# Mixture of experts beside a recurrent scan on one core: gate and up weights made the stationary operand, 256 rows of one expert at a time, loops written out

## What is computed

```python
xn = layernorm(x)
# branch 1: recurrent scan over each sequence
xk, xv, xr = (xn * m + shift(xn) * (1 - m) for m in (mix_k, mix_v, mix_r))
k, v, r = xk @ Wk.T, xv @ Wv.T, sigmoid(xr @ Wr.T)
s = (r * wkv_scan(time_decay, time_first, k, v)) @ Wo.T     # running max, numerator, denominator
# branch 2: 16 experts, 4 per token, FFN width 256
top_w, top_e = top_k(softmax(xn @ w_router.T), 4);  top_w /= sum(top_w)
ffn = sum over the 4 chosen experts e of
      top_w[e] * ((silu(xn @ w_gate[e]) * (xn @ w_up[e])) @ w_down[e])
out = x + s * silu(ffn)
```

## Time and profile before

| | us |
|---|---|
| median of 3 runs | 352.96 |
| the runs | 349.82, 352.96, 354.08 |
| span of the profiled execution | 358.9 |
| PE busy in it | 304.6 (85%) |
| DVE busy | 274.4 (76%) |
| POOL busy | 223.9 (62%) |
| ACT busy | 149.9 (42%) |

### The profile page before, as it was taken

One profiled execution on the slowest core, in us unless ns is written; L12 is line 12 of the kernel. 1 busy time (PEld: TensorE's weight loads), 2 busy tenths in 40 slices (PEclk: granted clock), 3 DMA queues, 4 the chain that ended last, 5 costly groups with the idle time before them and its releaser, 6 DMA issues.

```text
span 358.9 us, 4910 instructions
## 1 busy us (share of the span) xinstructions
PE 304.6 (85%) x1189; PEld 178.7 (50%) x1190; DVE 274.4 (76%) x531; ACT 149.9 (42%) x228; POOL 223.9 (62%) x229
## 2 busy tenths in 40 slices
PE   0998997898999999999979995999999989989000
PEld 0444443434465656565546562665656556678000
DVE  4788998589698696895867894598795961289993
ACT  1983762134534526327226326135517223254220
POOL 4400699957777677676756676367777752348254
PEclk9999999999999999999999999899999999999755
DMA  7899964213222224221214222024222489186123
GB/s 247 285 313 349 348 219 141 93 47 87 89 87 88 69 89 141 80 88 57 93 58 119 88 83 89 18 88 137 70 92 83 149 238 307 65 275 204 53 100 117
DMA packets 37862, 48.81 MB, mean 136 GB/s; under 512 B 3724, under 2 KB 33421, under 8 KB 37840
## 3 DMA queue, kind: packets, MB, share of 16 engines
q1 hardware_dynamic: 29600, 29.62, 25.6%
q0 software_dynamic: 7008, 18.10, 16.4%
q10 hardware_dynamic: 1232, 0.81, 0.7%
HBM read 35.94 MB, written 13.63 MB: 138 GB/s over the span
## 4 chain that ended last, share of the span: by engine, by line
PE 50%; DVE 21%; issue 10%; POOL 8%; ACT 3%; another core or an unknown queue 3%; DMA 2%; DVEq 0%; POOLq 0%; ACTq 0%
PE ps L571 40%; POOL ohB L342 7%; DVE wbig L1053 6%; PE ps L689 4%; PE ps L676 3%; PE ps L581 2%; DMA wrou<-wrouT_in 1%; ACT arena L535 1%; DVE arena L960 1%; DVE wbig L1068 1%; DVE arena L1008 1%; ACT L519 1%; DVE arena L965 1%; DVE wbig L1051 1%
## 5 line engine op out<-in xcount | busy, mean ns | idle before, releaser
L571 PE MATMUL ps<-wbig,arena 128*128 x576 | 204.1, 494 | 12.0 <-DVE arena L960 7.7
L571 PEld LDWEIGHTS ps<-wbig,arena 128*128 128x128 f32 x576 | 103.5, 192 | 75.9 <-issue 69.2
L385 POOL DMA_INDIRECT y_rows<-arena,s_idx x52 | 56.7, 1090 | 33.3 <-ACT arena L524 16.0
L378 POOL DMA_INDIRECT arena<-xn_rows,g_idx x56 | 62.0, 1108 | 19.6 <-issue 17.5
L519 ACT ACTIVATE arena<-ps 128x512 f32<-128x512 f32 x36 | 21.5, 597 | 86.8 <-PE ps L571 54.1
L965 DVE TENSOR_TENSOR arena<-arena,ps 128x512 f32<-128x512 f32 x36 | 24.6, 683 | 32.5 <-ACT arena L519 24.3
L342 POOL TENSOR_SCALAR ohB<-late 128x128 f16<-128x128 f32 x24 | 31.5, 1324 | 24.1 <-DVE late L869 24.1
L571 PE MATMUL ps<-arena 128*128 128x512 f32 x96 | 45.5, 608 | 0.4 <-DVE arena L808 0.4
L960 DVE COPY arena<-ps 128x512 f32<-128x512 f32 x36 | 24.9, 691 | 26.9 <-PE ps L689 14.9
L524 ACT COPY arena<-ps 128x512 f32<-128x512 f32 x36 | 21.0, 585 | 42.2 <-PE ps L571 34.7
L1053 DVE SCALAR_TENSOR_TENSOR wbig<-wbig,coef 128x256 f32<-128x256 f32 x36 | 28.8, 861 | 0.1
(11 more groups left out here) (144 smaller groups left out, 370.6 us busy)
## 6 DMA issues: line engine op xcount, KB each, us to landing
wbig<-y_rows SPq DMA_DIRECT2D x3, 2048.0 KB, 8.7
wbig<-wg_in SPq DMA_DIRECT2D x2, 2048.0 KB, 13.0
wbig<-wu_in SPq DMA_DIRECT2D x2, 2048.0 KB, 19.1
wbig<-wd_in SPq DMA_DIRECT2D x2, 2048.0 KB, 13.4
rT<-x_in SPq DMA_DIRECT2D x4, 512.0 KB, 6.6
xn_rows<-rT SPq DMA_DIRECT2D x4, 512.0 KB, 3.3
kT<-x_in SPq DMA_DIRECT2D x8, 256.0 KB
wbig<-y_rows SPq DMA_DIRECT2D x8, 256.0 KB, 5.4
```

The costliest lines, as they stand in the source:

```text
L378: pool.indirect_dma_start(out=xg[par][:, j, :], out_offset=None, in_=xn_rows, in_offset=bass.IndirectOffsetOnAxis(ap=idx[:, n + j:n + j + ...
L385: pool.indirect_dma_start(out=y_rows, in_=ysb[:, par, j, :], in_offset=None, out_offset=bass.IndirectOffsetOnAxis(ap=idx[:, n + j:n + j + ...
L571: ins = nc.tensor.matmul(dst, lhsT(c), rhs(c), start=(c == 0), stop=(c == C - 1))
```

## The change

The expert stage is written anew.

- The unit of work is 256 rows of one expert (`UNIT`), and experts are padded up to whole units. At least 32 units are needed and 33 are always run (`FIRST`); the rest stand in seven nested `If` blocks of two units (`optional`), so up to 47 are possible. One-hot tables become 94 slots wide instead of 80.
- Gate and up use slices of 128 x 128 weights as the stationary operand, and 256 transposed rows of the unit stream past. The result comes out with hidden channels on partitions, which is what `down` needs as its stationary operand. So `transpose_h` and `evac_h` go, and DVE's `hidden` writes `hT` itself.
- PE's order in a step i is: transpose rows of unit i, gate of unit i-1, down of unit i-2, up of unit i-1. Gate and up have semaphores of their own, so silu can start after the gate half.
- Gate and up weights are no longer held for all experts. ACT loads those of one unit's expert (512 KB, from an array laid out for it on the host) into one of two buffers, once for each unit, at the end of each step (`load_expert`), through an expert number that it reads into a register.
- PSUM: rows and results have two banks each (`XT_BANK`, `Y_BANK`).
- All loops are written out; the index copies, the register arithmetic for the loop and the `Fori` go. The scatters left at the end are those of six units instead of five pairs.

```diff
+UNIT = 2 * P
+NEED = ROWS // UNIT
+FIRST = NEED + 1
+BLOCKS = -(-(E - 2) // 2)
+NP = FIRST + 2 * BLOCKS
...
-            for half, src in ((0, wg_in), (1, wu_in)):
-                for c in range(C):
-                    sp.dma_start(wgu[:, :, c, half * D:(half + 1) * D],
-                                 src.rearrange("e (c p) n -> c p e n", p=P)[c]).then_inc(wgu_in, 16)
...
+            def load_expert(i):
+                wait(act, up_psum, i - 1)
+                expert = act.value_load(unit_expert[0:1, i:i + 1], min_val=0, max_val=E - 1)
+                act.dma_start(wgu[:, i % 2].rearrange("p c n -> p (c n)"),
+                              wgu_in[bass.ds(expert, 1)].rearrange("a p n -> p (a n)")).then_inc(wgu_loaded[i % 2], 16)
...
-            def gate_up(par, j, expert):
-                return product(ps[:, B_G + 2 * par + j, :], lambda c: xTg[:, par, j, c, :],
-                               lambda c: wgu[:, bass.ds(expert, 1), c, :].rearrange("p a n -> p (a n)"))
...
+            def half_of(i, par, half, free, done):
+                wait(pe, free, i - 1)
+                for h in range(C):
+                    at_n = half * D + h * P
+                    ins = product(ps[:, B_G + 2 * par + half, h * UNIT:(h + 1) * UNIT],
+                                  lambda c: wgu[:, par, c, at_n:at_n + P],
+                                  lambda c: xTg[:, par, c, :])
+                ins.then_inc(done, 1)
...
+            def step(i):
+                transpose_x(i)
+                if i > 0:
+                    gate(i - 1, (i - 1) % 2, 16 * ((i - 1) // 2 + 1))
+                if i == 2:
+                    pe.wait_ge(wdn_in, 16)
+                if i > 1:
+                    down(i - 2, i % 2, expert_of(i - 2))
+                if i > 0:
+                    up(i - 1, (i - 1) % 2)
...
-            def evac_h(i, par):
-                dve.wait_ge(ht_psum, i + 1)
-                wait(dve, y_psum, i - 1)
-                V.tensor_copy(hT[:, par].rearrange("p j c t -> p (j c t)"), ps[:, B_HT, :]).then_inc(ht_ready, 1)
-
             def hidden(i, par):
                 dve.wait_ge(sg_ready, i + 1)
-                wait(dve, ht_psum, i - 1)
-                V.tensor_tensor(hid[:, par], sg[:, par], ps[:, B_G + 2 * par:B_G + 2 * par + 2, D:2 * D], ALU.mult).then_inc(h_ready, 1)
+                dve.wait_ge(up_psum, i + 1)
+                wait(dve, y_psum, i - 1)
+                V.tensor_tensor(hT[:, par].rearrange("p h t -> p (h t)"), sg[:, par], ps[:, B_G + 2 * par + 1, :],
+                                ALU.mult).then_inc(h_ready, 1)
```

More of the change, by code:

```diff
@@ L290, in _ @@
                 sp.dma_start(y4[:, :, s, :], y_v[:, :, s, :]).then_inc(y_in[s], 16)
-            sp.wait_ge(y_psum, pairs)
-            for i in range(2):
-                sp.wait_ge(y_out[i], scattered)
+            sp.wait_ge(y_psum, units)
+            for par in range(2):
+                sp.wait_ge(y_out[par], scattered[par])
             for n in range(T // 2):
@@ L424, in _ @@
+            blocks, low = units_used(pool)
+            optional(pool, blocks, step)
+            first = pool.value_load(used[0:1, 2:3], min_val=2 * (FIRST - LAG), max_val=2 * (NP - LAG))
+            pool.tensor_copy(e_idx[:, :], dst_idx[:, bass.ds(first, 2 * LAG)]).then_inc(ei_ready, 1)
             pool.wait_ge(ei_ready, 1)
-            for n in range(LAG - 1):
-                scatter(last + n, (n + 1) % 2, e_idx, 2 * n)
+            for n in range(LAG):
+                scatter(low + n, (FIRST - LAG + n) % 2, e_idx, 2 * n)
@@ L526, in step @@
-            def step(o):
-                first = isinstance(o, int) and o == 0
-                for u in range(PAIRS):
-                    i = o * PAIRS + u
-                    evac_x(i + 1, (u + 1) % 2)
-                    if u % HALF == 1:
-                        piece = o * C + u // HALF
+                wait(act, y_out[par], scattered)
+                nc.scalar.copy(ysb[:, par].rearrange("p j n -> p (j n)"), ps[:, Y_BANK[par], :]).then_inc(y_ready, 1)
+            def step(i, blocks=None):
[3 more added lines that the diff above has]
+                        piece = (i - 1) // HALF
@@ L549, in _ @@
-            evac_y(last + LAG - 2, 1, last + LAG - 3)
+                    silu(i - 1, (i - 1) % 2)
[3 more added lines that the diff above has]
+                    next_expert(i + 1, blocks)
+            for i in range(FIRST - 1):
+                step(i)
+            act.wait_ge(slots_known, 3)
+            blocks, low = units_used(act)
+            step(FIRST - 1, blocks)
+            optional(act, blocks, lambda i: step(i, blocks))
@@ L735, in _, with transpose_x @@
-            outer_steps(pe, step)
-            blocks, last = pairs_used(pe)
-            for k in range(BLOCKS):
-                with pe.If(blocks > NEED // 2 + k):
-                    for i in (NEED + 2 * k, NEED + 2 * k + 1):
-                        pair(i, i)
-            experts = experts_of(last + LAG - 2)
-            transpose_h(last + LAG - 2, 1)
-            down(last + LAG - 2, 1, experts)
+            def transpose_x(i):
+                pe.wait_ge(xg_in[i % XG], 32 * (i // XG + 1))
+                wait(pe, xt_ready, i - 1)
+                for c in range(C):
+                    for j in range(2):
+                        ins = nc.tensor.transpose(ps[:, XT_BANK[i % 2], (c * 2 + j) * P:(c * 2 + j + 1) * P],
+                                                  xg[i % XG][:, j, c * P:(c + 1) * P], ident[:, :])
+                ins.then_inc(xt_psum, 1)
@@ new lines, in _ @@
+            pe.wait_ge(experts_ready, 1)
+            for i in range(FIRST):
+                if i == 1:
+                    pe.wait_ge(proj_out, BATCH * 3 * C)
+                step(i)
+            blocks, low = units_used(pe)
+            optional(pe, blocks, step)
+            gate(low + LAG - 1, (FIRST - 1) % 2, 16 * blocks + 16)
+            down(low + LAG - 2, FIRST % 2, expert_of(low + LAG - 2))
+            up(low + LAG - 1, (FIRST - 1) % 2)
+            down(low + LAG - 1, (FIRST - 1) % 2, expert_of(low + LAG - 1))
```

356 lines of the change are left out of this document (131 added, 225 removed).

## The result

| | before | after |
|---|---|---|
| median, us | 351.69 (4 runs, 349.82 to 354.08) | 365.62 (4 runs, 364.43 to 367.12) |
| ratio | | 1.0397, 95% interval 1.0329 to 1.0466 |
| profiled execution: span | 358.9 | 364.6 |

The changed kernel is slower by 14 us, about 4%. The forecast was 351.0, so even its sign was wrong. The profiled execution of the changed kernel took 366.68 us, 2 us beyond its span. The profiled execution of before has a span that is longer than any of its timed runs. That turns out to matter.

A forecast was written before the change was run, and what follows sets the result against it. PE's back-to-back expert-stage work was taken as the bound; start to 100.0, 34 steps 191.1, seven pieces 10.5, reads 1.5, then drain and tail gave span 356.9, scaled to 351.0 us; range 342 to 364.

The forecast's parts named there:

- the loop itself costs 12.5 - 1.8 = 10.7 us: Expert stage, pairs 8 to 24: 12.5 us lost against steady pace, less four scan pieces at 0.45 each.
- the same sum of 356.9: Whole kernel: start, steps, pieces, reads and tail add to span 356.9 us, 2.0 less than 358.9.
- part 1: PE's steady pace: hidden-row transposes go, products cost 0.216 us each, a step takes 5.62 us instead of 6.05.
- The rule on exposed weight loads: Gate and up on PE: 8 further unhidden loads add 1.5 us per unit, 60 us over 39 units; chance 0.01.
- part 2: Padding of experts to 256 rows: 36 pairs become 39 units, 217.8 us becomes 219.2, nothing won at steady pace.
- parts 3 and 4: Exponentials and per-unit weight loads on ACT: together 1.5 us lost per piece of the scan.
- part 3: Exponentials: hidden rows of a piece's second unit come late, PE stalls 1.1 us in each of 8 pieces.
- The 0.4 for the late load: Step with exponentials: weight load queued behind them on ACT lands at 13.15, gate wants it at 12.8.
- They meet the 2048 KB result loads near the end: Argument for the late-weights rival, weight loads landing after gate wants them: 362 to 421 us; chance 0.20.
- part 4: Per-unit weight loads: landing taken as 3.7 us, hidden in ordinary steps up to 5.1, 0.4 us more with exponentials.
- The rival's price, 4.75 to 6.57 us: Fetch-stall rival: one long jump out of the nested blocks costs this once, 356 to 358 us; chance 0.06.
- part 5: POOL's gathers: 5.6 us per unit against PE's 5.97, so POOL just keeps up; index copies go.

The follow-up runs named there:

- the second: The kernel before, unchanged, run again for another profiled execution: 351.04 us, ratio 1.0021, profiled span 350.2.
- both: Changed kernel with units fixed at 39 and ACT's exponentials behind silu and the result's copy, result loads whole: 352.17 us, ratio 0.9999.
- both, with the blocks kept: Changed kernel, nested blocks kept, ACT's exponentials behind silu and result copy, slot 0's 2048 KB result load in quarters: 353.47 us, ratio 0.9998.

## Why the prediction was wrong

1. **The baseline, 8.7 us: the largest error.** The step is "the loop itself costs 12.5 - 1.8 = 10.7 us". That number came from one execution, and the second has 99.45 for 109.29. Written out, the old kernel gains 1.5 to 2.2 us by its ratios. The text noticed that the timed runs were 4.8 to 9.1 us shorter, but made it a side note and scaled by proportion. The sum itself has no term for the loop; the 10.7 came in through the 358.9 that it was set against. Against a span of 350.2 the same sum of 356.9 would have been a loss of 1.9%. Why the first execution stalled at the loop's edges stays open: the one block fetched in that stretch doesn't settle it, as both profiles of before have the same 10 packets on that queue (q14), two of them between 160 and 230 us in either. The Trainium skill (Runtime: NRT & Kernel Launch, Instruction fetch mechanics) says that a taken branch out of the fetched pages stalls the engine for a fetch; with the loop this case shows long waits at its edges in one profiled execution and none in the other.
2. **The pace (part 1) held**: 5.62 us, 936 records. The rule on exposed weight loads doesn't hold here: a load takes 192 ns beside products of 216 ns and PE doesn't slow down. The section of the Trainium skill that the prediction cites for it (TensorE: Matmul & The Clock Gate, The mechanism) also lets a load run ahead when it goes to the background weight buffer, which the prediction left out.
3. **Padding (part 2) held** as arithmetic: 39 units eat the transposes removed.
4. **Exponentials and load (parts 3 and 4)**: forecast 1.5 us a piece, measured 1.40. But the parts of it differ. PE waits 1.14 us, the 1.1 of part 3. The 0.4 for the late load came as no wait; instead the products behind the idle take 0.27 more. With the exponentials moved, the load went out while they still ran: on ACT's queue it stands behind waits and register loads, not behind the activation's 1.91 us.
5. **Landing of the weights**: 3.9 in the median against 3.7 taken, 3.2 at best. The Trainium skill's fit for DMAs from GpSimd (DMA: Bandwidth & Descriptors, Anatomy of one DMA), an estimate of 3.2 for 512 KB, agrees with the shortest.
6. **The meeting with the 2048 KB load: 6.4 us that the sum didn't have.** "They meet the 2048 KB result loads near the end" stood among the reasons of a rival, without a price or a place. A step covers a landing of 5.1 us by part 4, so the 8.7 that these weights took leave a wait of 8.7 - 5.1 = 3.6; the idle was 3.48, and the rest of the 6.4 is mostly half clock. That the earlier trace rows also gives 8.7 us, for the 2048 KB load, is chance: the one met here took 13.3. The Trainium skill (DMA: Bandwidth & Descriptors, Queues, rings and completion order) says that DMA engines take turns between queues packet by packet. The trace shows such sharing from 288 on; from 284.9 to 288 SP's queue has 1004 of the 1005 packets moved, though the weights had been issued at 284.21. Why they start so late stays open.
7. **The drain**: 15.3 us from the last transpose to the end of `hidden` for the 11.7 reckoned, and 11.75 with 39 fixed units. So what the sum lacked there goes with the blocks and the reads that they need. Two waits of 1.26 and 1.22 us are in it, next to a branch out of the blocks that takes 4.86 us on PE's sequencer (three others take under 0.1), as the row for the comparing branches of L242 shows (min, median, max in ns):

```profile
L242 PEldq COMPARE_BRANCH  x4: 65/77/4862, 269.5 to 308.9; - x4
```

   The rival's price, 4.75 to 6.57 us, was right for the branch itself; half of it was hidden.
8. **The start**: step 4 at 99.24, forecast 100.0. **POOL** (part 5) kept up. **The tail** grew by 0.6 us.

Absolute, the sum of 356.9 missed the span of 364.6 by 7.7: 3.5 up to step 38 (6.4 for the meeting, less 0.8 at the start, 0.7 over the pieces and 1.5 of reads that didn't show), 3.6 in the drain, 0.6 in the tail. With the 8.7 of the baseline that is the miss.

## What to carry to other kernels

A profiled execution that lies outside its own timed runs is no baseline: what is peculiar to it, here 10 us at a loop's edges, goes into the sum as if the change could win it, so reckon both ways or with the steady part alone. When an order is turned around, move the work that filled an engine's idle stretch along with the stretch; the same move won 13 us in one order and lost 23 to 25 in the other. When per-step loads are added, look for the largest transfer that starts just ahead of one of them, and give the meeting a price and a place in the sum: here loads of 512 KB behind one of 2048 KB landed after 7.4 to 9.1 us instead of 3.9, and what the step doesn't cover of that is a wait.

## What the runs showed of the hardware

- A 512 KB load issued 1.1 us behind a 2048 KB load on another queue landed after 8.7 us instead of 3.9, and the larger after 13.3 instead of 8.5. Its own queue moved nothing for the first 3.8 us. In three more kernels that have this meeting (39 fixed units; exponentials moved; both) the smaller took 8.9, 7.4 and 9.1 us, the larger 13.4, 10.5 and 13.5.
- After an idle of 3.48 us PE's granted clock was 0.50 from 293 to 296; the wait cost 6.4 us in all. After an idle of 2.13 us it stayed at 1.00. An idle of 1.14 us cost 0.27 us more, at a granted clock of 1.00.
- A DMA issue on ACT's queue went out at 137.97 while the activation ahead of it ran from 137.49 to 139.40.
- A jump out of nested blocks took PE's sequencer 4.86 us in the changed kernel and 3.87 to 5.11 in three others; PE's waits in the drain around it differ, from 1.0 us (exponentials moved) over 2.5 (the changed kernel) to 5.7 (both, with the blocks kept).
